# Two key stacks with earlier sends, and a later reciprocal and normalisation, in a three-layer transformer kernel

## The chip, the cores and the metric

The kernel runs on one core of a Trainium2 chip. A core has five engines with a queue of instructions each: TensorE (PE, matmuls, with its weight loads listed as PEld), VectorE (DVE), ScalarE (ACT), GpSimd (POOL) and SyncE (SP, which only starts transfers here). They wait for each other through semaphores. The metric is the device time of one execution in microseconds; lower is better.

## The reference

16 samples of 256 tokens with 288 channels first pass a rotation (L0), then three transformer layers (L1 to L3) of the same form with their own weights. One layer, with layer norm without parameters and a modulation from the condition vector:

```python
ada = silu(c) @ W_ada + b_ada            # six vectors of 288 per sample
h = ln(x) * (1 + scale_a) + shift_a
qkv = h @ W_qkv + b_qkv                  # 16 heads of 18 channels
attn = softmax(q @ k.T * 18 ** -0.5)     # 256 x 256 per head
x = x + gate_a * ((attn @ v) @ W_proj + b_proj)
h = ln(x) * (1 + scale_f) + shift_f
x = x + gate_f * (gelu(h @ W_fc1 + b_fc1) @ W_fc2 + b_fc2)   # 1152 hidden channels
```

## The kernel before

**Tiling.** After the rotation (`prepare`, the first 165 us or so), `layers` runs 48 half steps, one for each sample of each layer (`it = 16 * l + b`). A half step is not one sample's work: it holds the second half of attention of sample `it` (shifted scores, exponentials, weighted values, normalisation), the projection and MLP of sample `it - 1`, the query, key and value tiles and the first scores of sample `it + 1`, and the norm of `it + 2`. Matmul operands are kept as a high and a low part, so each converted tile is a copy (high) and a subtraction (low); POOL does many of the low parts.

**Heads and stacks.** The 16 heads are handled as 8 units of two heads, units 0 to 7. The query and key tiles in `qk` come out of the matmul in an order that doesn't suit the scores, so small transfers within SBUF rearrange them into `q_stack` and `k_stack`, each with 8 units: 15 transfers for the queries on SP's queue (`stacks`) and 12 for the keys on POOL's (`first_keys` for units 0 to 4, `last_keys` for units 5 to 7). There is one stack of each, so the sends for sample `it + 1` must wait until the shifted scores (`shifted_units`, which also read the stacks) of sample `it` are done: units 0 to 4 for the first sends, all for the last.

**Scores and softmax.** PE computes scores of two units at a time into the two buffers `scores` (`score_units`), DVE takes the row maxima of each unit (`unit_max`), and the next two units wait for those maxima. In the following half step the negated maxima go in as one more row of `q_stack` and `shifted_units` computes the scores again, transposed and shifted, for ACT's exponentials. `v_sb` has a column of ones, so the sums come out of the weighted values. They take a way through DRAM: ACT stores them (`gather_sums`), loads them back more densely (`load_sums`), DVE takes the reciprocal (`inverse`), ACT stores it (`store_inverse`) and loads it spread over the partitions (`spread_inverse`), DVE multiplies (`normalise`), then ACT makes the high and POOL the low part of `o_att`, which the projection of the next half step needs.

**Order.** Each engine's order is written out by hand in its own `half_step`. On PE, after `values`, it is: up 0 to 2, scores of units 0 and 1, up 3 and 4, transposes, scores of units 2 and 3, down (two parts), scores of 4 and 5, down, scores of 6 and 7, down; the next half step opens with the projection. On ACT it is: gelu 0 and 1, `load_sums`, the value tile, gelu 2, `store_inverse`, gelu 3, two of the four spread loads, gelu 4, the other two, the high parts of `o_att`, the modulation for `it + 2`. On DVE the reciprocal stands ahead of all maxima. On POOL, after the attention sum and the small root of the norm: the low part of `h_mlp`, the root of the norm of `it + 2`, the keys, the low parts of `hidden`, of `o_att`, the output sum, and the low part of `h_att` for `it + 2`. In the half steps with `b` = 0 and 1 and 15, weight conversions for the layer stand in between.

**Loops.** An outer loop runs over the layers and an inner one over the samples from 2 to 13, one half step each round; the others stand in the code on their own.

The lines that set the keys' waits before:

```python
pool.wait_ge(s_qk_lo, QK_USES * it + QK_USES)   # all three key and query tiles split
if not first:
    pool.wait_ge(s_st, 8 * it - 3 + PRE)        # shifted scores 0 to 4 of the sample before
```

## Time and profile before

| | |
|---|---|
| time, median of 3 runs | 2189.09 us (2180.36 to 2191.14) |
| the profiled execution | 2181.43 us, span 2179.7 us |
| mean granted TensorE clock | 0.956 |
| busy share | PE 89%, DVE 55%, ACT 54%, POOL 53% |
| PE idle before scores of the stacks (L1840) | 95.4 us |
| plain half steps (35; b from 2 to 14, without those of the next line) | 39.2 us on average, from start to start of the maxima's transposes |
| half steps that start at 688.5, 1339.0 and 1948.9 us | 42.2, 42.9 and 43.5 us |
| half steps with b = 0 (854.5 and 1503.9 us) | 46.6 and 44.6 us |
| half steps with b = 15 (809.6 and 1459.8 us) | 44.9 and 44.1 us |
| filling `k_stack` once, on ACT (L369) | 1.89 us, at 15.8 us |

In the rows below, the timeline gives start, duration, engine, line, operation and operands, the count of merged instructions, and in brackets how long the engine sat idle before and what released it. "ACTq" is a transfer being issued on ACT's queue.

### The profile page before, as it was taken

To read this page: it belongs to the slowest core of one execution; us is meant where nothing else is said; L and a number is where in the kernel's file an instruction comes from. 1 tells how busy PE (TensorE), PEld (TensorE's weight loads), DVE (VectorE), ACT (ScalarE), POOL (GpSimd) and SP (SyncE) were. 2 spreads that over 40 slices of the span, in tenths; PEclk is the share of its full clock that TensorE was granted. 3 is DMA by queue.
4 is the path that set the end of the run, shared out by engine and by line. 5 is a ranking of instruction groups with operands and counts; after the bars stand their busy time and mean duration, and the time that the engine had idled before them with its cause. 6 is when DMAs were issued, how large, how long until landed. Compare 5 with 4: busy or idle time off the path is not lost. (4 is left out here: it accounts for less than half of the span.)

```text
span 2179.7 us, 51741 instructions
## 1 busy us (share of the span) xinstructions
PE 1946.7 (89%) x17367; PEld 1652.0 (76%) x17367; DVE 1202.7 (55%) x2735; ACT 1172.5 (54%) x2026; POOL 1163.0 (53%) x1511
## 2 busy tenths in 40 slices
PE   5785689999999898889999999999799999999987
PEld 2554578888888787678888888787678888888876
DVE  6883555455455575555465464574565455554641
ACT  3333455656556555555656556555555556555553
POOL 1003555655555555755655655656655656555543
PEclk9896799999999999999999999999999999999998
DMA  6432433323323333433323323233323323333220
GB/s 181 118 119 86 145 94 87 98 75 101 94 68 106 86 86 97 145 93 83 101 76 94 101 81 100 79 89 108 123 76 92 101 70 106 85 90 94 75 77 25
DMA packets 113198, 207.41 MB, mean 95 GB/s; under 512 B 46213, under 2 KB 62723, under 8 KB 112047
## 3 DMA queue, kind: packets, MB, share of 16 engines
q1 hardware_dynamic: 62766, 127.30, 20.8%
q0 software_dynamic: 25296, 49.71, 8.0%
q10 hardware_dynamic: 25040, 29.18, 4.8%
q8 instruction: 53, 0.87, 0.2%
q14 instruction: 43, 0.34, 0.0%
HBM read 99.51 MB, written 20.82 MB: 55 GB/s over the span
## 5 line engine op out<-in xcount | busy, mean ns | idle before, releaser
L2088 DVE TENSOR_REDUCE maxima<-scores 128x4 f32<-128x1024 f32 x384 | 449.5, 1213 | 91.0 <-PE scores L1840 90.9
L1903 PE MATMUL mlp_ps<-h_mlp,w_up 128*128 128x256 f32 (+1 forms) x3024 | 421.8, 291 | 29.6 <-ACT hidden L1662 26.0
L1903 PEld LDWEIGHTS mlp_ps<-h_mlp,w_up 128*128 128x128 f32 (+1 forms) x3024 | 377.3, 191 | 72.3 <-ACT hidden L1662 34.6
L1614 ACT ACTIVATE probs<-scores 128x1024 f32<-128x1024 f32 x384 | 372.4, 1023 | 82.7 <-PE scores L1864 79.4
L1754 PE MATMUL mlp_ps<-w_down,hidden 128*128 128x288 f32 x2592 | 395.5, 306 | 0.0
L1754 PEld LDWEIGHTS mlp_ps<-w_down,hidden 128*128 128x128 f32 x2592 | 365.6, 195 | 12.2
L1395 POOL TENSOR_TENSOR hidden<-g_full,hidden 128x512 fp32r<-128x512 f32 (+1 forms) x240 | 278.9, 1174 | 153.6 <-ACT hidden L1662 152.6
L1283 POOL DMA_DIRECT2D k_stack<-qk x576 | 295.5, 528 | 30.1 <-issue 18.8
L2093 DVE RECIPROCAL inv_few<-sums 128x32 f32<-128x32 f32 x48 | 16.9, 353 | 452.9 <-DMA sums<-sum_scratch 452.9
L1840 PE MATMUL scores<-k_stack,q_stack 54*128 54x256 f32 x1536 | 149.0, 315 | 95.4 <-DVE maxima L2088 73.1
L1661 ACT ACTIVATE g_full<-mlp_ps 128x512 f32<-128x512 f32 (+1 forms) x240 | 133.3, 555 | 162.1 <-issue 56.4
L1395 POOL TENSOR_TENSOR o_att<-o_full,o_att 128x512 fp32r<-128x512 f32 x96 | 121.8, 1290 | 173.5 <-ACT o_att L1638 173.5
L1840 PEld LDWEIGHTS scores<-k_stack,q_stack 54*128 54x128 f32 x1536 | 109.0, 195 | 134.4 <-DVE maxima L2088 82.7
L1395 POOL TENSOR_TENSOR h_mlp<-h_full,h_mlp 128x512 fp32r<-128x512 f32 x48 | 72.3, 1507 | 246.4 <-DVE h_mlp L2054 246.2
L1878 PE MATMUL pv_ps<-probs,v_sb 128*32 128x256 f32 x3072 | 200.9, 391 | 0.8 <-ACT probs L1614 0.8
L1754 PE MATMUL mlp_ps<-w_out,o_att 128*128 128x288 f32 x1152 | 172.7, 300 | 1.7 <-issue 1.7
L1754 PEld LDWEIGHTS mlp_ps<-w_out,o_att 128*128 128x128 f32 x1152 | 158.9, 191 | 3.1 <-issue 2.1
L1864 PE MATMUL scores<-q_stack,k_stack 55*128 55x256 f32 x1536 | 146.1, 310 | 4.5 <-ACT probs L1614 3.1
L1604 ACT ACTIVATE neg_max<-att_ps 16x256 fp32r<-16x256 f32 x48 | 18.0, 374 | 234.5 <-PE att_ps L1850 234.5
L1864 PEld LDWEIGHTS scores<-q_stack,k_stack 55*128 55x128 f32 x1536 | 106.4, 190 | 49.2 <-ACT probs L1614 29.5
L1811 PE MATMUL att_ps<-h_att,w_in 128*108 128x256 f32 (+3 forms) x1008 | 137.4, 284 | 5.8 <-POOL h_att L1395 5.1
L1878 PEld LDWEIGHTS pv_ps<-probs,v_sb 128*32 128x32 f32 x3072 | 86.0, 111 | 67.0 <-issue 12.9
(230 smaller groups left out, 2921.1 us busy)
## 6 DMA issues: line engine op xcount, KB each, us to landing
q_stack<-qk SPq DMA_DIRECT2D x288, 90.0 KB
k_stack<-qk POOLq DMA_DIRECT2D x288, 90.0 KB, 3.2
inv_sum<-inv_scratch ACTq DMA_DIRECT2D x192, 128.0 KB, 2.6
k_stack<-qk POOLq DMA_DIRECT2D x288, 54.0 KB, 3.5
x_mid<-out_x SPq DMA_DIRECT2D x48, 288.0 KB, 4.2
out_x<-x_out SPq DMA_DIRECT2D x48, 288.0 KB, 3.1
x_in<-out_x SPq DMA_DIRECT2D x47, 288.0 KB, 4.0
q_stack<-qk SPq DMA_DIRECT2D x144, 54.0 KB
```

What stands on the lines that cost most here:

```text
L1283: engine.dma_start(stack[first:first + HD, units, :].bitcast(F32), qk[part][row:row + HD, src, :].bitcast(F32)).then_inc(signal, 16)
L1395: tt(out, full, high.bitcast(F32), ALU.subtract).then_inc(signal, 1)
L1604: evict(neg_max[:, :], att_ps[0:H, 0:T], ACT.Copy, scale=-1.0).then_inc(s_neg, 1)
L1614: evict(probs[:, u % 4, :, :, :], scores[u % 2][:, :, :, :], ACT.Exp, scale=SCALE)\
L1661: evict(g_full[:, n % 2, 0:width], bank[:, 0:width], ACT.Gelu_apprx_tanh).then_inc(s_gelu, 1)
L1754: last = mm(out, a(left), c(weights[w]), start=start and n == 0, stop=stop and n == total - 1)
L1811: last = mm(qk_bank[n][0:cols.stop - cols.start, (m % 2) * T:(m % 2 + 1) * T], w[:, cols], h, start=count == 0, stop=count == 6)
L1840: last = mm(scores[v % 2][:, par, qt, :], q_stack[r, v, qt * P:(qt + 1) * P], k_stack[r, v, :], start=True, stop=True, tile_position=(R * ...
L1864: last = mm(scores[v % 2][:, par, kt, :], k_stack[r, v, kt * P:(kt + 1) * P], q_stack[r, v, :], start=True, stop=True, tile_position=(R * ...
L1878: last = mm(pv_ps[32 * i:32 * i + 32, (g % 2) * T:(g % 2 + 1) * T], v_sb[:, kt, 4 * g + i, :], probs[:, u % 4, i % 2, kt, :], start=kt == ...
L1903: last = mm(up_bank[n % 2][:, (m % 2) * T:(m % 2 + 1) * T], w[:, m * P:(m + 1) * P], h, start=count == 0, stop=count == 6)
L2088: nc.vector.tensor_reduce(out=maxima[:, :, :, u].rearrange("p q r -> p r q"), in_=scores[u % 2][:, :, :, :], axis=AX.X, op=ALU.max).then_i ...
```

## The change

1. `k_stack` gets a second copy; samples with an odd number use one, those with an even number the other. Each `half_step` takes the parity as an argument, and the inner loop's body now holds two half steps (`2 * n` and `2 * n + 1`, n from 1 to 6), since parity must be known when the program is written.
2. `first_keys` and `last_keys` no longer wait for shifted scores. `first_keys` stands ahead of `mlp_low` on POOL; `last_keys` stays behind the root of the norm of `it + 2`.
3. On DVE the reciprocal stands behind the maxima of units 0 and 1, the normalisation behind units 4 and 5 (it was behind 2 and 3), and the first gated down product ahead of unit 7 (it was ahead of 6).
4. The fill of the key stack in the preparation covers both copies.

```diff
-        k_stack = sb("k_stack", [P, H // 2, T], F32R)
+        k_stack = sb("k_stack", [P, 2, H // 2, T], F32R)
...
+            def loop(l):
+                half_step(l, 1, 1)
+                with engine.Fori(1, B // 2 - 1) as n:
+                    half_step(l, 2 * n, 0)
+                    half_step(l, 2 * n + 1, 1)
+                half_step(l, B - 2, 0)
+                half_step(l, B - 1, 1)
+
             prologue()
-            half_step(0, 0)
+            half_step(0, 0, 0)
             with engine.Fori(0, L - 1) as l:
-                half_step(l, 1)
-                with engine.Fori(2, B - 2) as b:
-                    half_step(l, b)
-                half_step(l, B - 2)
-                half_step(l, B - 1)
-                half_step(l + 1, 0)
...
+                loop(l)
+                half_step(l + 1, 0, 0)
+            loop(L - 1)
             epilogue()
...
+                if after:
+                    first_keys(it + 1, 1 - odd)
                 if before:
                     mlp_low(it - 1)
                 if after_next:
                     inverse_deviation(0, it + 2)
                 if after:
-                    first_keys(it + 1)
-                    last_keys(it + 1)
+                    last_keys(it + 1, 1 - odd)
...
                 pool.wait_ge(s_qk_lo, QK_USES * it + QK_USES)
                 pool.sem_inc(s_tick[1], 1)
-                if not first:
-                    pool.wait_ge(s_st, 8 * it - 3 + PRE)
-                    pool.sem_inc(s_tick[1], 1)
...
-                if not first:
-                    pool.wait_ge(s_st, 8 * it + PRE)
-                    pool.sem_inc(s_tick[1], 1)
...
-                inverse(it)
                 if at(b, 1):
                     convert_weights(l, OF["b_down"], "down")
                 for u in range(8):
-                    if u == 4:
+
+                    if u == 2:
+                        inverse(it)
+                    if u == 6:
                         normalise(it)
-                    if u == 6 and before:
+                    if u == 7 and before:
                         gate_down(it - 1, 0)
                     if after:
                         unit_max(it + 1, u)
```

How it stands on the engines. POOL in the inner loop, from the low part of `h_mlp` on, before:

```order
L1509 ISA
L1395 TENSOR_TENSOR h_mlp<-h_full,h_mlp 128x512
L1387 ISA
L1390 TENSOR_SCALAR rstd<-mean_var 128x2
L1391 REGISTER_ALU
L1392 TENSOR_TENSOR rstd<-rstd,minus_half 128x2
L1490 ISA
L1493 ISA
L1283 DMA k_stack<-qk 18x1280 x6
L1502 REGISTER_ALU
L1283 DMA k_stack<-qk 18x768 x6
```

The same place in the change (its line numbers are a few off):

```order
L1492 ISA
L1284 DMA k_stack<-qk 18x1280 x6
L1505 ISA
L1396 TENSOR_TENSOR h_mlp<-h_full,h_mlp 128x512
L1388 ISA
L1391 TENSOR_SCALAR rstd<-mean_var 128x2
L1392 REGISTER_ALU
L1393 TENSOR_TENSOR rstd<-rstd,minus_half 128x2
L1284 DMA k_stack<-qk 18x768 x6
```

The first six sends moved ahead of `h_mlp`, and two waits are gone. DVE in the inner loop from the reciprocal to the normalisation (`maxima<-scores` is one unit's maximum, `o_full<-o_full,inv_sum` the normalisation), before:

```order
L2093 RECIPROCAL inv_few<-sums 128x32
L2084 ISA
L2088 TENSOR_REDUCE maxima<-scores0 128x2x2
L2084 REGISTER_ALU
L2088 TENSOR_REDUCE maxima<-scores1 128x2x2
L2084 REGISTER_ALU
L2088 TENSOR_REDUCE maxima<-scores0 128x2x2
L2084 REGISTER_ALU
L2088 TENSOR_REDUCE maxima<-scores1 128x2x2
L2096 ISA
L2100 TENSOR_TENSOR o_full<-o_full,inv_sum 128x512 x2
```

And in the change, from the reciprocal, behind which there are still four maxima:

```order
L2089 RECIPROCAL inv_few<-sums 128x32
L2080 REGISTER_ALU
L2084 TENSOR_REDUCE maxima<-scores0 128x2x2
L2080 REGISTER_ALU
L2084 TENSOR_REDUCE maxima<-scores1 128x2x2
L2080 REGISTER_ALU
L2084 TENSOR_REDUCE maxima<-scores0 128x2x2
L2080 REGISTER_ALU
L2084 TENSOR_REDUCE maxima<-scores1 128x2x2
L2092 ISA
L2096 TENSOR_TENSOR o_full<-o_full,inv_sum 128x512 x2
```

Ahead of it two more maxima stand now, those of units 0 and 1, so the normalisation has six maxima before it instead of four.

## Rows read from the trace of the kernel before

**Rows 1.** Waits: engine, line and what it waited for: us in total, times, longest.

```profile
PE scores L1840 <- DVE maxima L2088: 73.1, 47, 5.2
```

**Rows 2.** Timeline of PE in the plain half step from 1027 to 1068 us.

```profile
1040.26 1.93 PE L1903 MATMUL mlp_ps<-h_mlp,w_up 128*128 128x256 f32 x14
...
1048.66 0.74 PE L1840 MATMUL scores<-k_stack,q_stack 54*128 54x256 f32 x8
...
1054.26 0.74 PE L1840 MATMUL scores<-k_stack,q_stack 54*128 54x256 f32 x8 [1.28 <-DVE maxima L2088]
1055.17 0.40 PE L1912 MATMUL mlp_ps<-b_down,ones_l 128*128 128x288 f32 x1 [0.17 <-ACT hidden L1662]
...
1057.89 0.74 PE L1840 MATMUL scores<-k_stack,q_stack 54*128 54x256 f32 x8
...
1064.43 1.75 PE L1754 MATMUL mlp_ps<-w_out,o_att 128*128 128x288 f32 x12
```

**Rows 3.** Timeline of ACT, the same half step: the sums' store and load issued.

```profile
1044.75 0.53 ACTq L1628 DMA_DIRECT2D sum_scratch<-o_full  x1
...
1049.32 0.34 ACTq L1633 DMA_DIRECT2D sums<-sum_scratch  x1
```

**Rows 4.** Timeline of DVE, the same half step.

```profile
1034.83 0.41 DVE L2064 TENSOR_TENSOR qk<-att_ps,qk 126x256 fp32r<-126x256 f32 x1
...
1051.65 0.35 DVE L2093 RECIPROCAL inv_few<-sums 128x32 f32<-128x32 f32 x1 [9.43 <-DMA sums<-sum_scratch]
...
1054.81 2.36 DVE L2088 TENSOR_REDUCE maxima<-scores 128x4 f32<-128x1024 f32 x2 [0.60 <-PE scores L1840]
1057.52 1.29 DVE L2100 TENSOR_TENSOR o_full<-o_full,inv_sum 128x512 f32<-128x512 f32 x2 [0.36 <-DMA inv_sum<-inv_scratch]
```

**Rows 5.** Timeline of POOL, the same half step.

```profile
1038.22 1.52 POOL L1395 TENSOR_TENSOR h_mlp<-h_full,h_mlp 128x512 fp32r<-128x512 f32 x1 [5.46 <-DVE h_mlp L2054]
...
1041.06 6.05 POOL L1283 DMA_DIRECT2D k_stack<-qk  x12
...
1058.96 2.54 POOL L1395 TENSOR_TENSOR o_att<-o_full,o_att 128x512 fp32r<-128x512 f32 x2 [3.03 <-ACT o_att L1638]
...
1066.84 0.81 POOL L1486 TENSOR_TENSOR x_one<-x_mid,gated 128x288 f32<-128x288 f32 x1 [0.87 <-DVE gated L2108]
```

**Rows 6.** Timeline of DVE: reciprocals of the first and last plain half step.

```profile
317.89 0.35 DVE L2093 RECIPROCAL inv_few<-sums 128x32 f32<-128x32 f32 x1 [10.69 <-DMA sums<-sum_scratch]
...
2094.99 0.35 DVE L2093 RECIPROCAL inv_few<-sums 128x32 f32<-128x32 f32 x1 [14.31 <-DMA sums<-sum_scratch]
```

**Rows 7.** Timeline of ACT in the half step from 809 to 855 us (b = 15).

```profile
835.21 0.53 ACTq L1628 DMA_DIRECT2D sum_scratch<-o_full  x1
...
837.27 0.35 ACTq L1633 DMA_DIRECT2D sums<-sum_scratch  x1
```

**Rows 8.** Timeline of POOL in that half step: the key sends.

```profile
823.15 3.49 POOL L1283 DMA_DIRECT2D k_stack<-qk  x6
830.15 3.12 POOL L1283 DMA_DIRECT2D k_stack<-qk  x6 [3.52 <-PE scores L1864]
```

**Rows 9.** Timeline of DVE in that half step.

```profile
839.14 0.35 DVE L2093 RECIPROCAL inv_few<-sums 128x32 f32<-128x32 f32 x1 [12.85 <-DMA sums<-sum_scratch]
```

**Rows 10.** Timeline of POOL in the half step that starts at 1339.0 us.

```profile
1361.87 2.00 POOL L1283 DMA_DIRECT2D k_stack<-qk  x4 [5.14 <-issue]
```

**Rows 11.** Timeline of PE in that half step.

```profile
1366.38 1.86 PE L1903 MATMUL mlp_ps<-h_mlp,w_up 128*128 128x256 f32 x7 [3.45 <-ACT hidden L1662]
```

**Rows 12.** Timeline of PE from 854 to 902 us: b = 0, and the outer loop's jump.

```profile
882.14 1.10 PE L1903 MATMUL mlp_ps<-h_mlp,w_up 128*128 128x256 f32 x7 [3.71 <-ACT hidden L1662]
...
899.39 1.85 PE L1754 MATMUL mlp_ps<-w_out,o_att 128*128 128x288 f32 x12 [1.65 <-issue]
```

**Rows 13.** Two neighbouring half steps: us, busy time by engine, granted clock, DMA.

```profile
489.00:527.68 38.68, 36.95 (x336) 31.94 (x335) 21.38 (x40) 23.01 (x38) 23.00 (x30) 1.00 0.33 92
527.72:567.90 40.18, 38.40 (x335) 33.44 (x334) 21.46 (x40) 23.01 (x38) 23.00 (x30) 0.96 0.32 88
```

More of the change, by code:

```diff
@@ L368, in constant_stacks @@
                     .then_inc(early["s_init"], 1)
-                A(k_stack[:, :, :].rearrange("p u t -> p (u t)"), one[:, 0:1].to_broadcast([P, H // 2 * T]), ACT.Copy)\
+                A(k_stack[:, :, :, :].rearrange("p n u t -> p (n u t)"), one[:, 0:1].to_broadcast([P, H * T]), ACT.Copy)\
                     .then_inc(early["s_kinit"], 1)
@@ L1246, in whole_run @@
         def whole_run(engine, prologue, half_step, epilogue):
+            def loop(l):
[5 more added lines that the diff above has]
+                half_step(l, B - 1, 1)
             prologue()
-            half_step(0, 0)
+            half_step(0, 0, 0)
             with engine.Fori(0, L - 1) as l:
-                half_step(l, 1)
-                with engine.Fori(2, B - 2) as b:
-                    half_step(l, b)
-                half_step(l, B - 2)
-                half_step(l, B - 1)
-                half_step(l + 1, 0)
-            half_step(L - 1, 1)
-            with engine.Fori(2, B - 2) as b:
-                half_step(L - 1, b)
-            half_step(L - 1, B - 2)
-            half_step(L - 1, B - 1)
+                loop(l)
+                half_step(l + 1, 0, 0)
+            loop(L - 1)
             epilogue()
@@ L1348, in prologue, with half_step @@
                 negated_maxima(0)
-            def half_step(l, b):
+            def half_step(l, b, odd):
                 it = l * B + b
@@ L1437, in prologue, with half_step @@
                 pool.wait_ge(s_kinit, 1)
-                first_keys(0, first=True)
-                last_keys(0, first=True)
+                first_keys(0, 0)
+                last_keys(0, 0)
                 low_weights("w_out", 0)
                 attention_low(1)
-            def half_step(l, b):
+            def half_step(l, b, odd):
                 it = l * B + b
@@ L1840, in score_units @@
                             last = mm(scores[v % 2][:, par, qt, :], q_stack[r, v, qt * P:(qt + 1) * P],
-                                      k_stack[r, v, :], start=True, stop=True, tile_position=(R * par, 0))
+                                      k_stack[r, odd, v, :], start=True, stop=True, tile_position=(R * par, 0))
                     last.then_inc(s_score, 1)
@@ L1863, in shifted_units @@
                             r = slice(R * par, R * par + HEAD_ROWS + 1)
-                            last = mm(scores[v % 2][:, par, kt, :], k_stack[r, v, kt * P:(kt + 1) * P],
+                            last = mm(scores[v % 2][:, par, kt, :], k_stack[r, odd, v, kt * P:(kt + 1) * P],
                                       q_stack[r, v, :], start=True, stop=True, tile_position=(R * par, 0))
@@ L1937, in prologue, with half_step @@
                 for u in range(0, 8, 2):
-                    score_units(0, u)
-            def half_step(l, b):
+                    score_units(0, u, 0)
+            def half_step(l, b, odd):
                 it = l * B + b
@@ L1961, in half_step @@
                 weighted_values(it, 0)
-                shifted_units(it, 4)
+                shifted_units(it, 4, odd)
                 weighted_values(it, 1)
@@ L1967, in half_step @@
                     values(it + 1, 0)
-                shifted_units(it, 6)
+                shifted_units(it, 6, odd)
                 m = it - 1
@@ L2145, in prologue, with half_step @@
                     unit_max(0, u)
-            def half_step(l, b):
+            def half_step(l, b, odd):
                 it = l * B + b
```

24 lines of the change are left out of this document (12 added, 12 removed).

## The prediction

> **What bounds the kernel now.** I read the waits by engine pair first, then the timelines of one plain half step, then the half steps that differ from it. TensorE is busy 89% of the span (table) and is the engine that the others wait for, so only its idle time can be won back. Its largest wait inside the layers is the scores' wait for the maxima, 73.1 us in 47 pieces [rows 1]. All of the 73 looks winnable, since at that point VectorE is not working: it stands at the reciprocal, which waits for the softmax sums to come back from DRAM.
>
> The plain half step from 1027.4 to 1066.0 shows the order of events. The scores of units 0 and 1 start at 1048.66; the next scores could start at 1052.98 but wait 1.28 us for maxima [rows 2]. VectorE does its first maxima only after the reciprocal at 1051.65 [rows 4]. But right behind the scores, the first down matmul starts at 1055.17 and it too has waited, for the last gelu on ScalarE [rows 2]. ScalarE's last gelus stand behind the store of the reciprocal, so **two chains leave the same reciprocal** and reach TensorE together: maxima to scores, and reciprocal to gelus to down, the latter 1055.17 - 1051.65 = 3.52 us long. Taking the maxima out of the first chain leaves the second. That decides this case.
>
> Why does the reciprocal come so late? The sums are stored at 1044.75 and the load is issued only at 1049.32, 4.57 us later [rows 3], while POOL sends twelve key pieces from 1041.06 to 1047.11 [rows 5]. In the half step at 810, whose last keys were sent by 833.27 [rows 8], the same store took 837.27 - 835.21 = 2.06 us [rows 7], and the reciprocal followed at 839.14, 1.87 us after the load's issue [rows 9]. So without key traffic beside it the sums would be there 3.93 us after the store, at 1048.7 here.
>
> **The change, part by part, in a plain half step (35 of the 48).** *Keys earlier.* The first six sends now follow the last key tile (1035.24 [rows 4]) and the last six follow POOL's small root, so all are issued 3 us before the sums' store. The sums then land about 1048.7, no longer the bound. *Reciprocal later.* It now stands behind the maxima of units 0 and 1. Unit 0's maximum starts 0.55 us after its scores (1054.81 against 1054.26) and two take 2.36, of which the reciprocal can overlap the last 0.08: it starts at 1048.66 + 2.83 = 1051.49. It was at 1051.65: the gain is only 0.16 us here. Over the 35 plain half steps the same difference runs from -0.24 to 1.24, mean 0.35 (the first and the last of the 35 reciprocals are [rows 6], 25.7 and 25.3 us after their half step's start, where this one is at 24.3). The down matmul stays 3.52 us behind the reciprocal, so the waits for maxima vanish, and come back as a wait of 1.3 us for the gelu. Gain: 0.35 us, not 1.3.
>
> *Normalisation later.* It stood ahead of units 4 and 5; now it stands behind them. Their scores start 2.72 us after the down matmul (1057.89 - 1055.17), the maxima end 0.55 + 2.27 later, so the normalisation starts 5.54 us after down; before it was 2.35. From its start to POOL's last low part of the attention output is 1061.50 - 1057.52 = 3.98 us [rows 4, 5]; that end moves from 6.33 to 9.52 us after down. The projection needs it 1064.43 - 1055.17 = 9.26 us after down: a **new wait of 0.3 us**. Behind it POOL's queue (output sum, next sample's low part, attention sum) is pushed from a state with 0.87 us of idle before the attention sum at 1066.84 [rows 5]; about 0.4 us of lateness passes into the norm and from there to the MLP transposes. I take 0.2 us, with bounds 0 and 0.5.
>
> *Sends ahead of the MLP's low part.* Six sends of 0.50 us (6.05 / 12 [rows 5]) beginning at 1035.3 end near 1038.4, where h_mlp began at 1038.22; it lasts 1.52 us and up needs it at 1040.26 [rows 2]. The slack of 0.52 covers it at 0.50 per send. At 3.49 / 6 = 0.58, the price of sends beside VectorE's work [rows 8], the slack is nearly used: 0.05 us, bounds 0 and 0.4.
>
> Plain sum: -0.35 + 0.3 + 0.2 + 0.05 = +0.2 us, times 35: **+7 us**. Against this, TensorE's clock: two neighbouring half steps of 38.68 and 40.18 us differ in nothing but a granted clock of 1.00 against 0.96 [rows 13], part of the down matmuls running at the 1.2 GHz level after the waits. Eight of 35 show this 1.5 us, most after a wait of 1.6 us or more. With the wait steadied at 1.3 I let four go: **-6 us** (bounds -12 and +46, below).
>
> *Half steps that differ.* (a) Three times POOL's queue itself stands still for 5.1 us within the last six sends [rows 10], and TensorE loses 3.45 us plus slower matmuls behind it [rows 11]; these half steps last 42.9 us on average against 39.2 for the plain ones (table of the profile). Sent 3 us sooner, the same standstill ends at about the usual time of the first gelu's low part: **-10 us** (bounds -12, and +4 if the standstill moved into the first six sends). (b) The two half steps with w_out's low parts behind the keys on POOL wait 3.71 us at up [rows 12], and their spread reciprocals come late; they last 46.6 and 44.6. With POOL 3 us earlier: **-10 us** (bounds -4, -12). (c) The last sample of a layer (twice) has no such waits now, its reciprocal starting about with the scores. There the later reciprocal costs some 1.6 us of gelu delay, plus the rest above, some 2.5 us in all: **+5 us**. (d) For the three half steps where POOL is late at h_mlp, six sends (3.1 us) stand in front, but bias conversion no longer delays the maxima: 0, bounds -4 and +9. (e) The first half step, without an MLP: -2 us. (f) Filling twice the stack is 1.9 us more of one ScalarE instruction in the first 20 us (table), ahead of idle time on that engine: nothing, or 1.9 us if that cover failed.
>
> Sum: 7 - 6 - 10 - 10 + 5 - 2 = **-16 us**. The profiled execution took 2181.4, which gives 2165; the median of the runs is 7.7 us higher, which gives 2173. I say 2170.
>
> **A rule against this change.** Six sends by POOL beside VectorE took 3.49 us, and six alone took 3.12 [rows 8]. The Trainium skill, "SBUF — State Buffer", section "SBUF: two separate sides", says that while VectorE runs a fast fp32 copy within SBUF, GpSimd is locked out and can't write descriptors; the trace agrees in direction, with 0.37 us for six. The first sends now stand beside exactly such copies (h_mlp), which makes it rival 2.
>
> **Rivals.** *1. Everything in the plain half steps is returned* by knock-on at its upper bound and clock drops that stay: 35 x 0.3 + 6 = +16, net 0, time 2186: "same". For it: POOL has under 1 us of slack. Against it: 0.5 needs both waits to add up. *2. The key sends are held up by VectorE's copies:* at twice the delay seen, six take 3.12 + 0.74 us, h_mlp starts 1.0 us later than now, and after the slack of 0.52 and the shift above up waits some 0.35 us: 35 x 0.35 = +12, net -4, time 2182: "same". *3. The loop's doubled body makes the jump back visible.* Now the jump over one half step costs TensorE nothing, while the jump over five costs 1.65 us [rows 12]. A body of two half steps jumps 15 times: +25, net +9, time 2195: "same", near the edge. The Trainium skill, "Runtime: NRT & Kernel Launch", section "Instruction fetch mechanics", gives TensorE room for 2048 instructions and a stall for a jump outside; a half step has 671 matmuls and loads [rows 13], so by that rule two still fit and the term is 0, as I take it. *4. Slower: clock drops in most half steps.* TensorE's idle time now comes in three pieces per half step, 1.3 + 0.3 + 0.2 us, instead of about 1.5 in all. If the clock then drops in all 35 instead of the four I left, +46, net +30, time 2216. From 18 more drops on it decides (27 us). Against it: it fell mostly after waits of 1.6 us. *5. The change doesn't do what it says:* if the query pieces, which SyncE still sends from a single stack, and not the keys, slow the sums, the sums stay at 24.5 and the reciprocal waits as before: 0.35 x 35 = +12, net -4, time 2182. The half step at 810 speaks against it, having query pieces too.
>
> **Chances.** Forecast 0.47, rival 1 0.14, rival 2 0.10, rival 3 0.06, rival 4 0.09, rival 5 0.05, a larger gain (the clock never drops, no knock-on: -32 us) 0.09. A measurement of this kernel tells about 0.5% (11 us) from no change. Some of rival 1's and 3's cases pass +11. That makes faster 0.52, same 0.35, slower 0.13. The range from the larger gain to the edge of the slower case is 2150 to 2198; the forecast's own range is 2158 to 2180.
>
> **What would show it.** Right: the wait scores <- maxima gone to under 10 us, a wait of the first down matmul for the gelu grown to some 45 us; the sums' load issued about 2 us after their store; the reciprocal 2.8 us after the scores; projection waiting 0.3 us for o_att; the half steps of (a) within 2 us of a plain one. Wrong: down starting straight behind the scores (then the gain is 40 us larger), h_mlp late for up, "issue" idle at every second projection (rival 3), a mean clock below 0.95 (rival 4).

## The result and the profile after

The changed kernel takes 2231.6 us (median of four runs, 2230.8 to 2243.9) against 2185.9 for the kernel before: a ratio of 1.022, 95% interval 1.018 to 1.027. It is **slower**, by about 46 us, where 2170 was forecast and 2198 was the end of the range. The profiled execution took 2231.4 us, span 2229.5 (before 2181.4 and 2179.7), and the mean granted clock is 0.944 (before 0.956).

TensorE's waits by engine pair, in the changed kernel (us in total, times, longest). The line numbers are four below those of before: L1836 is the scores of the stacks, L1899 up, L1908 the first matmul of a down group, L1750 projection and down.

```profile
PE mlp_ps L1908 <- ACT hidden L1658: 76.5, 48, 3.2
PE mlp_ps L1899 <- POOL h_mlp L1396: 25.5, 41, 3.4
PE mlp_ps L1750 <- POOL o_att L1396: 18.6, 38, 6.4
...
PE scores L1836 <- DVE maxima L2084: 12.3, 8, 2.0
```

The wait for maxima fell from 73.1 us [rows 1] to 12.3, and the gelu's wait in front of down rose to 76.5. The second line is new and was not forecast at this size: up waits for the low part of `h_mlp` in nearly every half step.

The same plain half step as [rows 2 to 5], in the middle of the second layer, from 1045.97 to 1086.96. TensorE:

```profile
1059.43 1.90 PE L1899 MATMUL mlp_ps<-h_mlp,w_up 128*128 128x256 f32 x14 [0.43 <-POOL h_mlp L1396]
...
1067.78 0.73 PE L1836 MATMUL scores<-k_stack,q_stack 54*128 54x256 f32 x8
...
1071.80 0.74 PE L1836 MATMUL scores<-k_stack,q_stack 54*128 54x256 f32 x8
...
1074.12 0.40 PE L1908 MATMUL mlp_ps<-b_down,ones_l 128*128 128x288 f32 x1 [1.58 <-ACT hidden L1658]
1074.36 4.08 PE L1750 MATMUL mlp_ps<-w_down,hidden 128*128 128x288 f32 x18
...
1085.27 1.85 PE L1750 MATMUL mlp_ps<-w_out,o_att 128*128 128x288 f32 x12 [0.20 <-POOL o_att L1396]
```

ScalarE's transfers, VectorE and POOL in that half step:

```profile
1063.89 0.53 ACTq L1624 DMA_DIRECT2D sum_scratch<-o_full  x1
1067.60 0.35 ACTq L1629 DMA_DIRECT2D sums<-sum_scratch  x1
```

```profile
1053.49 0.41 DVE L2060 TENSOR_TENSOR qk<-att_ps,qk 126x256 fp32r<-126x256 f32 x1
...
1068.33 2.36 DVE L2084 TENSOR_REDUCE maxima<-scores 128x4 f32<-128x1024 f32 x2 [6.78 <-PE scores L1836]
1070.60 0.34 DVE L2089 RECIPROCAL inv_few<-sums 128x32 f32<-128x32 f32 x1
```

```profile
1054.51 3.37 POOL L1284 DMA_DIRECT2D k_stack<-qk  x6 [2.89 <-DVE qk L2060]
1057.89 1.30 POOL L1396 TENSOR_TENSOR h_mlp<-h_full,h_mlp 128x512 fp32r<-128x512 f32 x1
...
1060.26 3.15 POOL L1284 DMA_DIRECT2D k_stack<-qk  x6
```

VectorE now stands idle for 6.78 us until the scores, although the sums are soon there: behind the two maxima the reciprocal starts at once, with no bracket. It starts 2.82 us after the scores and down 3.52 us after it, as the prediction had worked out. The second scores (1071.80) wait for nothing. What is new: a wait of 1.58 us in front of down, and **behind it a block of 18 down matmuls of 4.08 us**. The next two half steps show what that is (start to end, us, busy times of PE, PEld, DVE, ACT and POOL, granted clock, DMA share, GB/s):

```profile
1086.96:1127.90 40.94, 38.64 (x337) 33.56 (x334) 21.33 (x40) 23.00 (x38) 23.13 (x31) 0.96 0.30 87
```

```profile
1127.90:1168.20 40.30, 37.19 (x336) 32.00 (x334) 21.32 (x40) 23.00 (x38) 23.11 (x31) 1.00 0.32 88
```

And the wait and the block of down matmuls in the second of them:

```profile
1156.87 0.40 PE L1908 MATMUL mlp_ps<-b_down,ones_l 128*128 128x288 f32 x1 [1.56 <-ACT hidden L1658]
1157.11 2.56 PE L1750 MATMUL mlp_ps<-w_down,hidden 128*128 128x288 f32 x18
```

Behind nearly the same wait the block takes 2.56 us here and 4.08 above. The same work keeps TensorE busy 1.45 us longer at 0.96 than at 1.00: part of it ran at the 1.2 GHz level instead of 2.4. I count a half step as one with a fall where its granted clock is under 0.985. That is so in 7 of the 35 plain half steps of before (the prediction counted 8, by their length) and in **23 of 35** after. Such a count is from one execution of each kernel, and executions of one kernel differ: on one chip the kernel before ran with mean granted clocks from 0.942 (2206.8 us) to 0.960 (2174.6 us). The four executions of the changed kernel lie at 0.936 to 0.944, around and below the lowest of these, so the extra falls aren't those of a single execution.

Where the 47 us went, from start to start of the maxima's transposes, summed by kind of half step:

| half steps | before, mean | after, mean | sum of the difference | forecast |
|---|---|---|---|---|
| 33 plain | 39.21 | 40.40 | +39.0 | +1 (all 35) |
| 2 plain with b = 14, layers 1 and 2 | 39.31 | 43.41 | +8.2 | in the line above |
| 3 with POOL's standstill | 42.88 | 40.42 | -7.4 | -10 |
| 2 with b = 0 | 45.63 | 42.61 | -6.1 | -10 |
| 3 with b = 1 | 46.89 | 49.47 | +7.7 | 0 |
| 2 with b = 15 | 44.52 | 47.37 | +5.7 | +5 |
| the first | 43.18 | 42.51 | -0.7 | -2 |

In the plain ones without a fall the half step went from 38.89 to 39.51 us, which is 35 x 0.62 = 22 us. The 16 further falls, at about 1.6 us (41.12 against 39.51), are another 26. The two half steps with b = 14 are counted among these falls; about 5 of the 26 us are what they lose beyond an ordinary fall. Without them a half step with a fall takes 40.90 us, so the fall alone costs about 1.4.

### The profile page after: what moved, and what is told of

The parts are those of the page before. It is cut to its first block and busy times, and to the rows that moved or that the text cites. A ratio compares the mean times of both kernels' runs of the same rounds, so it can differ in the third digit from the quotient of the medians.

```text
span 2229.5 us, 51288 instructions
## 1 busy us (share of the span) xinstructions
PE 1974.0 (89%) x17367; PEld 1677.8 (75%) x17367; DVE 1200.8 (54%) x2735; ACT 1173.4 (53%) x2026; POOL 1170.3 (52%) x1511
## 5 line engine op out<-in xcount | busy, mean ns | idle before, releaser
L2084 DVE TENSOR_REDUCE maxima<-scores 128x4 f32<-128x1024 f32 x384 | 455.9, 1219 | 548.1 <-PE scores L1836 548.1
L1899 PE MATMUL mlp_ps<-h_mlp,w_up 128*128 128x256 f32 (+1 forms) x3024 | 413.8, 290 | 30.0 <-POOL h_mlp L1396 25.5
L1899 PEld LDWEIGHTS mlp_ps<-h_mlp,w_up 128*128 128x128 f32 (+1 forms) x3024 | 375.5, 191 | 68.5 <-issue 51.0
L1750 PE MATMUL mlp_ps<-w_down,hidden 128*128 128x288 f32 x2592 | 421.6, 319 | 0.0
L1750 PEld LDWEIGHTS mlp_ps<-w_down,hidden 128*128 128x128 f32 x2592 | 389.5, 207 | 12.3 <-issue 0.2
L1284 POOL DMA_DIRECT2D k_stack<-qk x576 | 315.4, 556 | 154.9 <-DVE qk L2060 145.4
L1634 ACT ACTIVATE o_att<-o_full 128x512 fp32r<-128x512 f32 x96 | 59.2, 632 | 273.1 <-DVE o_full L2096 273.1
L1750 PE MATMUL mlp_ps<-w_out,o_att 128*128 128x288 f32 x1152 | 180.2, 308 | 19.8 <-POOL o_att L1396 18.6
L1750 PEld LDWEIGHTS mlp_ps<-w_out,o_att 128*128 128x128 f32 x1152 | 160.6, 194 | 31.7 <-issue 26.9
L1836 PE MATMUL scores<-k_stack,q_stack 54*128 54x256 f32 x1536 | 148.4, 313 | 23.5 <-DVE maxima L2084 12.3
L1836 PEld LDWEIGHTS scores<-k_stack,q_stack 54*128 54x128 f32 x1536 | 108.7, 195 | 58.1 <-issue 25.1
L1807 PEld LDWEIGHTS att_ps<-h_att,w_in 128*108 128x108 f32 (+3 forms) x1008 | 129.6, 182 | 11.2 <-issue 6.6
L1658 ACT ACTIVATE hidden<-mlp_ps 128x512 fp32r<-128x512 f32 (+1 forms) x240 | 133.7, 557 | 0.0
```

Of the source, the lines that this page charges most:

```text
L1284: engine.dma_start(stack[first:first + HD, units, :].bitcast(F32), qk[part][row:row + HD, src, :].bitcast(F32)).then_inc(signal, 16)
L1658: evict(hidden[0][:, tiles, :].rearrange("p a t -> p (a t)"), bank[:, 0:width], ACT.Gelu_apprx_tanh)\
L1750: last = mm(out, a(left), c(weights[w]), start=start and n == 0, stop=stop and n == total - 1)
L1807: last = mm(qk_bank[n][0:cols.stop - cols.start, (m % 2) * T:(m % 2 + 1) * T], w[:, cols], h, start=count == 0, stop=count == 6)
L1836: last = mm(scores[v % 2][:, par, qt, :], q_stack[r, v, qt * P:(qt + 1) * P], k_stack[r, odd, v, :], start=True, stop=True, tile_position= ...
L1899: last = mm(up_bank[n % 2][:, (m % 2) * T:(m % 2 + 1) * T], w[:, m * P:(m + 1) * P], h, start=count == 0, stop=count == 6)
```

## The experiments

All were timed against the kernel before on the same chip (2188.0, 2188.6 and 2189.4 us in the three groups). This table is the key to them: waits are TensorE's, us per plain half step, from the one profiled execution of each; "falls" as above. Two waits aren't in it. In the kernels whose keys are sent late (before, 1, 5 and 7) the first scores also wait 0.18 to 0.23 us per half step for the last keys themselves (7.2 us in all in the kernel before). Early sends take this wait away, a gain that the prediction left out. And in kernels 9, 10 and 12 the last group of up waits 0.43 to 0.53 us for a gelu.

| kernel | median | ratio, 95% | down for gelu | up for h_mlp | scores for maxima | falls of 35 | mean without a fall |
|---|---|---|---|---|---|---|---|
| before | 2185.9 | 1 | 0.17 | 0 | 1.26 | 7 | 38.89 |
| changed | 2231.6 | 1.022 (1.018, 1.027) | 1.63 | 0.47 | 0.06 | 23 | 39.51 |
| 1: loop only | 2196.8 | 1.005 (1.001, 1.008) | 0.26 | 0 | 1.30 | 14 | 38.72 |
| 2: normalisation back | 2212.4 | 1.010 (1.006, 1.014) | 1.62 | 0.48 | 0.05 | 23 | 38.99 |
| 3: reciprocal first | 2147.0 | 0.979 (0.974, 0.984) | 0.16 | 0.48 | 0.41 | 0 | 38.54 |
| 4: keys only | 2127.1 | 0.972 (0.967, 0.976) | 0.17 | 0.45 | 0.38 | 1 | 37.94 |
| 5: VectorE's order only | 2226.5 | 1.018 (1.012, 1.025) | 1.61 | 0 | 0.01 | 9 | 39.47 |
| 6: reciprocal behind one unit | 2154.8 | 0.984 (0.980, 0.989) | 0.71 | 0.47 | 0.04 | 1 | 38.61 |
| 7: 4 with keys behind h_mlp | 2211.3 | 1.009 (1.006, 1.012) | 0.29 | 0 | 1.33 | 10 | 39.09 |
| 8: 4 with small queries | 2105.0 | 0.962 (0.957, 0.967) | 0.08 | 0.47 | 0.16 | 2 | 37.46 |
| 9: 4 with sends 4 + 8 | 2161.3 | 0.985 (0.980, 0.990) | 0.26 | 0 | 0.78 | 1 | 38.56 |
| 10: changed, sends 4 + 8 | 2188.1 | 1.000 (0.997, 1.003) | 1.24 | 0 | 0 | 2 | 39.28 |
| 11: 4, outer loop unrolled | 2117.3 | 0.965 (0.960, 0.970) | 0.18 | 0.45 | 0.39 | 0 | 37.96 |
| 12: 9 and 11 | 2143.9 | 0.976 (0.971, 0.981) | 0.30 | 0 | 0.79 | 2 | 38.62 |

**1. The loop alone** (the kernel before with a body of two half steps, one key stack, the old order).

```diff
-                with engine.Fori(2, B - 2) as b:
-                    half_step(l, b)
+                with engine.Fori(1, B // 2 - 1) as n:
+                    half_step(l, 2 * n)
+                    half_step(l, 2 * n + 1)
```

> The kernel before with the changed kernel's loop alone: a body of two half steps, one key stack, old order on POOL and VectorE. Theory (the loss of 46 us comes from the later reciprocal and the clock that falls behind its new wait): the loop costs little, 2186 to 2198 us; a few us for the outer loop's jump, since its body is six half steps and not five. Rival (the doubled body makes instructions late on some engine in each round): 2215 to 2232 us.

Measured 2196.8 us, 1.005 times before, so some 9 us for the loop. The inner jump costs TensorE nothing: the plain half steps without a fall last 38.72 us, before 38.89. (Its clock fell more often, 14 times, but the profiled execution is the longest but one of ten, 2207.7 us at a clock of 0.942 where the others reach 0.954.) Some of the time is lost where the outer loop jumps back. The half step with b = 0 in front of that jump lasts 50.0 us (46.6 before), the one with b = 1 behind it 51.2 (46.6). POOL stands without a releaser behind the jump, which it did not in the kernel before:

```profile
916.99 1.54 POOL L1486 TENSOR_TENSOR x_one<-x_mid,gated 128x288 f32<-128x288 f32 x2 [3.80 <-issue]
```

The other half steps with b = 0 and 1 have no such jump; two of the three are longer as well, by 2.6 and 3.9 us, for which no cause is shown. Rival 3 is refuted in its mechanism (15 jumps of 1.65), but a third of its price is there, in part at the outer jump and on another engine.

**2. The normalisation and the gated product back** (in the changed kernel).

```diff
-                    if u == 6:
+                    if u == 4:
                         normalise(it)
-                    if u == 7 and before:
+                    if u == 6 and before:
                         gate_down(it - 1, 0)
```

> The changed kernel with the normalisation back behind units 2 and 3 and the first gated down product ahead of unit 6; the reciprocal stays behind units 0 and 1. Theory: only the projection's wait of 0.2 us goes, the wait of 1.56 us for the gelu and the clock's fall stay: 2218 to 2228 us. Rival (the late normalisation and its knock-on through POOL are the larger part): 2185 to 2205 us.

Measured 2212.4, some 6 us below the 2218 to 2228 expected, since more than the projection's 0.2 us came back. Without falls the plain half step is 38.99 instead of 39.51: 0.52 us each, 18 in all, and 19 is what the time shows. That is the 0.3 + 0.2 us of the prediction. The wait at down (1.62) and the 23 falls stayed: the reciprocal is another matter.

**3. The reciprocal back ahead of the maxima** (in the changed kernel; normalisation stays late).

```diff
                 for u in range(8):
-                    if u == 2:
+                    if u == 0:
                         inverse(it)
```

> The changed kernel with the reciprocal ahead of all maxima again; keys early and normalisation late as in the changed kernel. Theory: sums land about 23.9 us into a plain half step, 0.6 us sooner than before the change, so the down matmul starts at 27.5 instead of 28.1 and most clock drops vanish: 35 x (0.6 + 1.0) = 56 us off, 2170 to 2185 us. Rival (the early key sends themselves, beside VectorE's copies and ahead of h_mlp, are the larger part): 2205 us or more.

Measured 2147.0: a gain of 85 us where 47 to 62 were expected. The reciprocal moved from 24.74 to 23.63 us after the half step's start, the wait at down from 1.63 to 0.16, and no half step has a fall any more. This one statement's place turns the case.

**4. The keys alone** (the changed kernel with the whole order of VectorE as before).

```diff
-                    if u == 2:
+                    if u == 0:
                         inverse(it)
-                    if u == 6:
+                    if u == 4:
                         normalise(it)
-                    if u == 7 and before:
+                    if u == 6 and before:
                         gate_down(it - 1, 0)
```

> Two key stacks and early sends only, with the doubled loop: VectorE in the order of the kernel before. Theory: as the run before it, less the projection's wait of 0.2 us: 2160 to 2178 us, faster than the kernel before by 0.4 to 1.2%. Rival (early keys give nothing since the query pieces set the sums' way): 2185 to 2200 us, from the wait of 0.45 us for h_mlp.

Measured 2127.1, ratio 0.972: faster by 61 us and far below the 2160 to 2178 that I gave it. Its half step from 484.59, POOL, ScalarE's queue and VectorE:

```profile
493.08 3.38 POOL L1284 DMA_DIRECT2D k_stack<-qk  x6 [3.08 <-DVE qk L2060]
496.48 1.29 POOL L1396 TENSOR_TENSOR h_mlp<-h_full,h_mlp 128x512 fp32r<-128x512 f32 x1
...
498.84 3.15 POOL L1284 DMA_DIRECT2D k_stack<-qk  x6
```

```profile
502.48 0.53 ACTq L1624 DMA_DIRECT2D sum_scratch<-o_full  x1
505.62 0.35 ACTq L1629 DMA_DIRECT2D sums<-sum_scratch  x1
```

```profile
507.36 0.35 DVE L2089 RECIPROCAL inv_few<-sums 128x32 f32<-128x32 f32 x1 [7.23 <-DMA sums<-sum_scratch]
```

The last send is issued by 501.99, 0.49 us before the store. Issued isn't landed: from issue to landing the first and the last six take 2.7 and 3.0 us (last figure, median):

```profile
k_stack<-qk POOLq DMA_DIRECT2D x288, 90.0 KB, 2.7
k_stack<-qk POOLq DMA_DIRECT2D x288, 54.0 KB, 3.0
```

The sums come back 4.88 us after the store (in [rows 3, 4] 6.90), and with that the maxima's wait shrinks from 1.26 to 0.38 us without any return of it at down. The scores start at 506.27, so the reciprocal at 507.36 is 1.7 us ahead of the place that the change gives it.

**5. VectorE's order alone** (the kernel before, one stack, with the three statements of VectorE placed as in the change).

```diff
-                inverse(it)
...
+                    if u == 2:
+                        inverse(it)
-                    if u == 4:
+                    if u == 6:
                         normalise(it)
-                    if u == 6 and before:
+                    if u == 7 and before:
                         gate_down(it - 1, 0)
```

> The kernel before (one key stack, old loop, keys late) with VectorE's order of the changed kernel alone. Theory (the later reciprocal puts one wait of about 1.6 us ahead of down, the late normalisation adds 0.2 to 0.3 us at the projection, and the clock then falls in most half steps): 2215 to 2235 us, slower than before by 1.3 to 2.2%, with the first down matmul waiting 1.4 us or more for the gelu. Rival (VectorE's order only hurts together with the early key sends): 2185 to 2200 us.

Measured 2226.5 against 2188.6, within the span I gave. The clock fell in 9 half steps and not in most, but the profiled execution is the shortest of four (2213.6 us, clock 0.952); the longest took 2238.5 at 0.940, so at the median the falls were more. TensorE's first wait in its list:

```profile
PE mlp_ps L1912 <- ACT hidden L1662: 69.6, 43, 3.1
```

So with or without the second stack the new order gives some 2226 to 2232 us, and with or without the new order the second stack's worth differs completely: -61 us with the old order, +5 with the new. **The late reciprocal throws the keys' gain away**, and more.

**6. The reciprocal behind one unit** (in the changed kernel).

```diff
-                    if u == 2:
+                    if u == 1:
                         inverse(it)
```

> The changed kernel with the reciprocal behind unit 0 only, not behind units 0 and 1. It can start 23.4 us into the half step, and the sums land at about 23.6: so down waits some 0.4 us instead of 1.56. Theory (the length of the wait ahead of down decides whether the clock falls): 2135 to 2155 us, plain half steps at 38.0 to 38.5 us, falls rare. Rival (the clock falls by the number of waits, which stays three): plain half steps near 39.8 us, 2185 us or more.

Measured 2154.8, against 2147.0 in front of all maxima and 2231.6 behind two. TensorE still waits three times per half step (0.71, 0.47, 0.17), but the clock falls in one half step only. So the number of waits, which rival 4 went by, doesn't decide; the length of the one at down goes with the falls.

**7. The keys behind h_mlp again** (in kernel 4; two stacks, no waits for shifted scores, only the order on POOL).

```diff
-                if after:
-                    first_keys(it + 1, 1 - odd)
                 if before:
                     mlp_low(it - 1)
+                if after:
+                    first_keys(it + 1, 1 - odd)
```

> Early keys with VectorE's old order (the fastest so far), but the first six sends behind the low part of h_mlp on POOL, as in the kernel before. Theory: the wait of 0.45 us for h_mlp goes, and up to the sums' store everything is 0.45 us sooner; but the last sends now end at 19 us and not 17, beside the sums' store at 17.4, so the sums gain less: 2120 to 2140 us. If the overlap with the store matters as much as before the change: 2150 us or more. If not at all: 2110 us.

Measured 2211.3 where 2120 to 2140 was expected: a miss by 70 us, and slower than before. It is the other branch, 2150 us or more, that came true. The forecast had reckoned with the 0.45 us at up and little else. POOL's sends, ScalarE's store and load, and the scores that wait:

```profile
501.77 3.06 POOL L1284 DMA_DIRECT2D k_stack<-qk  x6
505.89 3.16 POOL L1284 DMA_DIRECT2D k_stack<-qk  x6
```

```profile
506.82 0.53 ACTq L1624 DMA_DIRECT2D sum_scratch<-o_full  x1
511.79 0.35 ACTq L1629 DMA_DIRECT2D sums<-sum_scratch  x1
```

```profile
516.84 0.74 PE L1836 MATMUL scores<-k_stack,q_stack 54*128 54x256 f32 x8 [1.39 <-DVE maxima L2084]
```

The last sends now lie on both sides of the store, the load comes 4.97 us after it (5.02 on average), and the wait for maxima is back at 1.33. Against kernel 4 the first six sends start 3.8 us later and the last are issued 2.2 us later. Two stacks without earlier sends are worth nothing.

**8. Query pieces of one row** (kernel 4; for every sample but the first, the nine later query transfers carry one row instead of 18, so the scores of units 5 to 7 are computed from stale queries. The number of transfers stays.)

```diff
+            def small_piece(j, par, part, src, row, units, whole):
+                first, rows = R * par + HD * j, HD if whole else 1
+                sp.dma_start(q_stack[first:first + rows, units, :].bitcast(F32),
+                             qk[part][row:row + rows, src, :].bitcast(F32)).then_inc(s_stack_b, 16)
```

> As the run with the early keys and VectorE's old order (2127 us), but the nine later query pieces of every sample but the first carry one row of 18 instead of all 18, so units 5 to 7 are computed from stale queries. Theory (the query pieces are what still keeps the sums' store at 3.7 us): the load is issued 2.1 to 2.6 us after the store instead of 3.7, the reciprocal starts at 22 us instead of 23.5, the last waits for maxima go: 2105 to 2118 us. Rival (the store takes 3.7 us by itself beside ScalarE's work): 2122 us or more.

Measured 2105.0, ratio 0.962. The load comes 3.22 us after the store (3.70 in kernel 4), not the 2.1 to 2.6 expected. So query traffic holds the sums up by 0.5 us. Another 1.2 us over the 2.06 of [rows 7] is left. The packets in the trace give a reason that no run of its own tested: keys issued just before the store are still moving behind it. In kernel 4 the last packet of POOL's queue ends 2.7 us after the store's issue on average, in kernel 8 2.2 us. In the half steps with b = 15 of the kernel before that is 0.1 us. The store's own packets end at 3.0, 2.4 and 1.75 us.

**9 and 10. Four sends ahead of h_mlp, eight behind the small root**, in kernel 4 and in the changed kernel.

```diff
-                for j in range(3):
+                for j in range(2):
                     for par in range(2):
                         head_into_stack(pool, k_stack[:, odd], j, par, ...)
...
+            def more_keys(it, odd):
+                for par in range(2):
+                    head_into_stack(pool, k_stack[:, odd], 2, par, ...)
...
                 if after:
+                    more_keys(it + 1, 1 - odd)
                     last_keys(it + 1, 1 - odd)
```

> The version with VectorE's old order and two key stacks (2127 us), with four of the first six key sends ahead of the low part of h_mlp and the other two behind POOL's small root. In that version the low part of h_mlp starts 3.38 us after the sends' start and up waits 0.45 us in a plain half step. My theory: two sends fewer in front give 1.1 us back, the wait of 0.45 us at up is gone, and the remaining eight sends (some 4.2 us) end where they ended before, 1.8 us ahead of the sums' store: 35 x 0.45 = 16, so 2105 to 2120. Rival: POOL and the small root are not what up waits for (it comes from the MLP transposes before), then up waits as before and the time is 2122 to 2130.

> The changed kernel (2231.6 us, up waiting 0.45 us for the low part of h_mlp) with the same division of sends, four ahead of h_mlp and two behind the root; VectorE's late reciprocal and normalisation stay. If the wait of 0.45 us was a loss of its own: 2212 to 2220. If the later reciprocal holds the half step's period whatever comes in front of it, being tied to the first scores, the scores themselves come 0.45 us sooner, and it still gains; only if the clock fell for that wait also would it gain more than 16 us. Under 5 us of gain would mean that the bound is the loop through the reciprocal, gelu, down and o_att alone.

In both the wait for `h_mlp` is gone and the scores start 0.5 us earlier in the half step (21.2 to 21.3, not 21.7 to 21.8). Behind the scores most of it is lost again: the last group of up waits 0.43 to 0.44 us for a gelu. The two results point in opposite directions. In kernel 4 the edit costs 34 us (2161.3): the eight sends and the store, one half step from 488.19:

```profile
501.77 4.15 POOL L1284 DMA_DIRECT2D k_stack<-qk  x8
```

```profile
505.58 0.53 ACTq L1630 DMA_DIRECT2D sum_scratch<-o_full  x1
510.02 0.35 ACTq L1635 DMA_DIRECT2D sums<-sum_scratch  x1
```

The sends end at 505.92, after the store's start and not 1.8 us ahead of it, as I had written (in kernel 4 they were 0.5 us ahead of it, never 1.8); the load is issued 4.44 us after the store here and 4.90 on average, and the wait for maxima doubles to 0.78. My expectation had forgotten that the store moves up by the 0.45 us won, too. It also ended the sends where they ended before; they end 0.4 us later in the half step.

In the changed kernel the same edit wins 43 us (2188.1, level with before), since the reciprocal behind two maxima hardly waits there for the sums (it starts 3.12 us after the scores, in the changed kernel 2.95). The 2212 to 2220 expected for a wait that is a loss of its own was too little. This is the clearest run on the clock: without falls the plain half step is only 0.23 us shorter (39.28 against 39.51, 8 us in all), but **falls went from 23 to 2**. All ten executions agree with that: their mean granted clocks are 0.952 to 0.963, those of the changed kernel 0.936 to 0.944. TensorE's waits in it:

```profile
PE mlp_ps L1914 <- ACT hidden L1664: 55.9, 43, 2.8
PE mlp_ps L1905 <- ACT hidden L1664: 26.3, 33, 2.5
```

The wait at down fell from 1.63 to 1.24 us, and up waits 0.43 us, now for a gelu, at a later group: one wait has become two. One of its two half steps with a fall, from 1027.39, looks like the one above:

```profile
1055.07 0.40 PE L1914 MATMUL mlp_ps<-b_down,ones_l 128*128 128x288 f32 x1 [1.58 <-ACT hidden L1664]
1055.30 4.07 PE L1756 MATMUL mlp_ps<-w_down,hidden 128*128 128x288 f32 x18
```

The length of the wait doesn't settle it: this kernel also has a half step with 2.76 us of wait at down and no fall. Across all runs, down's wait at 1.6 with h_mlp's 0.47 gave 23 falls (changed, 2), 1.6 alone 9 (5), 1.24 gave 2 (10), 0.7 and less 0 to 2 where maxima cost under 0.8, and a wait of 1.3 us for maxima gave 7 to 14 (before, 1, 7).

**11 and 12. The outer loop written out**, in kernel 4 and with the division of sends as well.

```diff
-            with engine.Fori(0, L - 1) as l:
+            for l in range(L - 1):
                 loop(l)
```

> The version with VectorE's old order and two key stacks (2127 us), with the outer loop over the layers written out, so that no jump back over a whole layer is left; the inner loop stays. In the changed kernel POOL stands 4 to 7 us without a visible cause behind that jump, and up waits for it. If the jump is the cause: the third half step of kind b = 1 loses its extra 2 to 4 us per jump, one or two jumps: 2119 to 2125. If POOL's stand comes from something else at the layer's start (its queue of transfers, the weights' arrival): 2125 to 2130.

> Both together: four of six sends ahead of h_mlp, and the outer loop written out. If the two gains are independent, their sum: 2098 to 2115. If one of them frees a queue that the other needs, the better one of the two alone.

Kernel 11 takes 2117.3, ratio 0.965 with interval 0.960 to 0.970: the fastest that computes everything, and 2 us below the 2119 to 2125 expected. Behind the jump in the changed kernel POOL and TensorE stand like this:

```profile
921.08 1.54 POOL L1488 TENSOR_TENSOR x_one<-x_mid,gated 128x288 f32<-128x288 f32 x2 [4.23 <-issue]
```

```profile
924.15 1.69 PE L1807 MATMUL att_ps<-h_att,w_in 128*126 128x256 f32 x7 [4.36 <-DVE qk L2060]
```

POOL waits for nothing that the profile shows, VectorE's query and key tiles wait for POOL's attention sum, and TensorE for them. That half step (b = 1 of layer 1) lasts 51.9 us in the changed kernel, 50.3 in kernel 4 and 43.7 in kernel 11, where POOL's idle is gone; before, with five half steps' code in the outer body, it lasted 46.6. So the jump is the cause; 6.6 us of it are seen in this one half step of kernel 11 and 10 us in the medians. Kernel 12 (2143.9) misses the expected 2098 to 2115 for the reason seen in 9, and confirms the jump's price once more: 17 us against kernel 9.

## Why the prediction was wrong, point by point

**What bounds the kernel, and the two chains: right.** Maxima's waits went, gelu's came; the reciprocal stood 2.82 us after the scores (forecast 2.83) and down 3.52 after it. The gelu's wait was 1.56 us in a typical half step, forecast 1.3.

**The step that failed is the clock's term.** The prediction put it at "-6 us", four falls fewer, since the wait would be "steadied at 1.3". It is +26 us: 16 falls more. That is 32 of the 62 us between the forecast gain of 16 and the measured loss of 46; the next largest is the 14 us below. In the trace of before 5 of the 7 falls had waits of 1.6 us or more for maxima. The forecast wait was set just below that bound, and came out at the bound (1.56 in a typical half step), with a second one of 0.45 us at up ahead of it. Rival 4 named this outcome, at 2216 and 0.09; it had the right effect and the wrong measure (the count of waits, which kernel 6 refutes). What makes the clock fall behind one wait of 1.56 us and not behind the next stays open. The term had both signs in its own bounds (-12 and +46), but the range of 2150 to 2198 left most of the upper one out.

**The low part of h_mlp: 0.45 us instead of 0.05, +14 us.** The bound of 0.4 was nearly right, the value not. Forecast: sends of 0.50 us begin 0.06 us after the last key tile, then `h_mlp` of 1.52, and 0.52 us of slack. In the rows above the sends begin 1054.51 - 1053.90 = 0.61 us after the tile, take 3.37 (for its 0.05 the prediction had used 3.49), `h_mlp` takes 1.30, and up starts 0.24 us after its end, so that much of the slack never was slack. Two terms were left out: 0.55 us of the sends' start and the 0.24 us between `h_mlp` and up. Against them stand 0.12 and 0.22 us by which the sends and `h_mlp` were shorter than reckoned. Rival 2's cause is in the wait too, though the 3.49 had it covered: the first six sends take 3.37 us ahead of `h_mlp`, and the same six 3.06 behind it in kernel 7. The Trainium skill, "SBUF — State Buffer", section "SBUF: two separate sides", says that GpSimd's descriptors wait while VectorE runs a fast fp32 copy; the trace agrees in direction, with 0.3 us for six.

**The sums' way: 3.66 us instead of 2.06.** The first half of the step held (keys sent sooner make it shorter than the 4.57 of [rows 3], 4.65 on average), the size didn't. What was wrong is "all are issued 3 us before the sums' store". The sends moved up by 3 us, from an end at 1047.11, and so by the prediction's own rows to some 0.6 us before the store at 1044.75; it is 0.48 us on average. In the reference, the half step with b = 15, the last keys were sent 1.94 us before the store [rows 7, 8] and had all but landed. Kernel 8 shows that query pieces are part of it as well. In the changed kernel this error cost nothing: the sums, due about 23.5 us after the start, were covered by the reciprocal's place at 24.7. In kernel 4 it leaves 0.38 us of wait.

**Normalisation and knock-on: right,** 0.3 + 0.2 forecast, 0.52 measured in kernel 2.

**b = 14 in layers 1 and 2: missed, +8 us** (3 of them are the two falls counted above)**.** VectorE converts weights there ahead of the maxima. Before, this delayed only the maxima. With the reciprocal behind them it delays the second chain too:

```profile
799.79 5.31 DVE L2076 TENSOR_TENSOR w_in<-staging,w_in 128x180 fp32r<-128x180 f32 x17
805.14 2.36 DVE L2084 TENSOR_REDUCE maxima<-scores 128x4 f32<-128x1024 f32 x2
807.52 0.35 DVE L2089 RECIPROCAL inv_few<-sums 128x32 f32<-128x32 f32 x1
```

```profile
811.04 0.40 PE L1908 MATMUL mlp_ps<-b_down,ones_l 128*128 128x288 f32 x1 [2.75 <-ACT hidden L1658]
```

Kernel 4, without that order, has 38.7 us here instead of 43.4. What a moved statement is moved behind has to be read in every kind of half step; the prediction read it in one.

**The half steps that differ.** The standstill (a) gave -7.4 for -10 (inside the sends POOL idles 2.3 to 2.9 us now, where it idled 5.1 to 5.4, and why it is shorter is open), b = 0 (b) -6.1 for -10, b = 15 (c) +5.7 for +5, so these three were right in sign. The three with b = 1 (d) gave +7.7 for 0, within their bounds of -4 and +9, but as a sum of unlike parts: +5.0 in layer 0, where up waits 2.58 us for `h_mlp` behind the sends; +5.3 in layer 1, where the prediction didn't have the outer jump's price on POOL; and -2.6 in layer 2.

**The trade between the two parts** was the deeper miss. The forecast said that the keys alone gain little, since "two chains leave the same reciprocal". That argument holds for a reciprocal at a fixed place. Kernel 4 moves it: 1.0 us earlier in the half step (24.53 to 23.52), and both chains gain together. The change then put the reciprocal back to 24.74.

## What to carry to other kernels

When a transfer is made to land sooner, look at who else leaves the same value, and leave its consumer where it can take the gain; moving that consumer back by what was won costs the gain and more. Where a statement moves behind others, read what else stands before those others in each kind of round. And price a new wait at both clock levels: here 0.4 us at each of two places went with 21 falls of about 1.5 us.

## What the runs showed of the hardware

- **Small differences in the waits went with large ones in the clock.** Kernel 10 and the changed one differ by 0.5 us at the first up and 0.4 us at down, with 0.4 us at the last up in their place, and have 2 and 23 falls of 35. A fall makes the 18 down matmuls behind the wait take 4.08 us instead of 2.56.
- **A few small transfers beside a round trip through DRAM hold it up.** From store to load: 2.06 us with no keys beside it [rows 7], 3.22 with small query pieces, 3.7 with the last send issued 0.5 us before (and not landed yet), 4.5 to 5.0 on average with the last sends issued beside or behind the store. Sending the last keys 2.2 us later, and the first 3.8, cost 84 us of time (kernels 4 and 7).
- **A jump back over a long body can cost POOL more than TensorE.** With six half steps' code in the outer body POOL idles without a releaser for 3.80 us in kernel 1, 4.23 in the changed kernel and 6.59 in kernel 3. With five, in the kernel before, POOL had no such idle and TensorE had 1.65 [rows 12]. A body of two half steps inside the inner loop shows none at its own jump.

What stays open: whether the store-to-load time would go down to 2.06 us with the keys landed before the store (no run sends them early enough, and query stacks in two copies don't fit into SBUF beside the rest, so this wasn't tried), and what beside the wait's length decides over a fall, since kernels 5 and 2 have the same 1.6 us at down and 9 and 23 falls (in part by which execution was profiled), and within the changed kernel 12 half steps of 35 wait about as long (1.40 to 1.80 us) and have none.
